# A spectral layer's mode mix split by image half and placed inside the passes of the other half, with one 112-column stationary operand for two image pairs

## The chip, the cores and the metric

The kernel runs on one core of one Trainium2 chip. The metric is the device time of one launch in microseconds (us), as the median of several runs. One further execution was taken with the hardware profiler; all rows below come from it.

## The reference

Four blocks act in turn on 32 images of 8 channels, 64x64: a coupled-map block with a small neural cellular automaton and a gate, a spherical 3x3 convolution, a spectral block (a grouped Fourier neural operator), and a second spherical convolution; the data are normalised between them. The change is almost all in the spectral block, which is this (40 channels, in 4 groups of 10):

```python
h = fc0(x)                                   # 2 channels and 2 coordinates of each group -> 10
for n in range(4):
    xf = jnp.fft.rfft2(h).reshape(Bb, G, WID, Hh, Wf)
    lo = jnp.einsum('bgixy,gioxy->bgoxy', xf[:, :, :, :M1, :M2], w1c)       # rows 0..11, 12 columns
    hi = jnp.einsum('bgixy,gioxy->bgoxy', xf[:, :, :, Hh - M1:, :M2], w2c)  # rows 52..63
    h = gswish(irfft2(lo and hi, zero elsewhere) + grouped 1x1 convolution of h)
out = fc2(gswish(fc1(h)))
```

## The kernel before, in words

`spectral_layers` does the Fourier transforms as matrix products. The 32 images are cut into 8 units of 4 images; a unit is 2 pairs (`S2`) of 2 images (`B2`). A pass is the work on one unit in one layer, and a layer is 8 passes. All five engines run their own written-out order of instructions and meet at semaphores. On TensorE a pass is:

- `pointwise` (L1380): 16 tiles of 4 matmuls. The stationary operand is 128 columns of `chan` (the transposed activations, and rows of the inverse transform in the other direction); the moving one is 96 columns of `cols`, which holds the row-transformed coefficients (partitions 0 to 47) and the 1x1 weights (48 to 127). So the inverse transform over the columns and the 1x1 convolution are one product. ScalarE evicts each tile with the activation (`activate`, L1480) into `act_b`, which has two buffers.
- `forward_rows` (L1434) of the unit before, put behind the first two tiles.
- `inverse_rows` (L1400) of the next unit: 10 tiles of 4 matmuls, each with 48 columns of `coef` (one channel of one image pair) as the stationary operand and `ih`, 128 columns, as the moving one. ScalarE copies each tile of 512 columns into `cols` (`cols_out`, L1489).
- `forward_cols` (L1414): 8 tiles of 5 matmuls, evicted by VectorE.

Every matmul on 32-bit floats stands in the trace as two records.

A layer's modes go to DRAM (`modes`) after each pass. When all 8 passes are done, `mix` (L1442) multiplies them with the weights of the layer: 8 chunks of 3 mode rows, 288 matmuls in all, with 40 stationary columns and 64 moving ones (two parts, 32 images). Even tiles are evicted by VectorE, odd ones by ScalarE, in four instructions each (`PARTS`), into one of two `om` buffers; SyncE stores these to DRAM (`mixed`), and a buffer is written again when its store has landed (`stored`). After the last store SyncE loads the first unit's `coef`, and the next layer begins. During this time SyncE also fills `cols` with the next layer's 1x1 weights by a broadcast transfer (L1338). The chunks of modes lie in the space of `act_b`, so mixing and passes cannot overlap:

```python
for layer in range(LAYERS):
    if layer:
        inverse_rows(layer, 0)
    for u in range(UNITS):
        ...
    forward_rows(layer * UNITS + UNITS - 1)
    pe.wait_ge(a_out, (layer + 1) * UNITS * NZ)
    for n in range(CHUNKS):
        mix(layer * CHUNKS + n)
```

`spectral_head` applies the last inverse transform, fc1 and fc2. A unit there is 16 tiles (`pointwise`, then `hidden` and `project` for earlier tiles); 10 of them also carry a tile of `inverse_rows` for the next unit. The head starts behind a barrier of all engines.

## Time and profile before

| what | us |
|---|---|
| median of 3 runs | 3396.33 |
| lowest and highest | 3392.22, 3400.08 |
| profiled execution, its own time | 3415.88 |
| its span in the trace | 3414.1 |
| TensorE, busy | 2765.8 (81% of the span) |
| VectorE, busy | 1928.0 (56%) |
| ScalarE, busy | 1436.8 (42%) |
| GpSimd, busy | 799.9 (23%) |

Busy time of TensorE counts pipelined matmuls and can overlap, so the distance from one start to a later one is what a group of matmuls costs. The granted clock is given in parts of 2.4 GHz: 1.00 is that, 0.50 is 1.2 GHz. TensorE's mean granted clock over the span is 0.921.

### The profile page before, as it was taken

The page shows a single profiled execution, that of the slowest core. Times are in us where ns is not written, and L with a number is a line of the kernel's source. Part 1 is how long each engine was busy: PE and PEld are TensorE (multiplying, and loading weights), DVE is VectorE, ACT ScalarE, POOL GpSimd, SP SyncE. Part 2 cuts the span into 40 slices and gives each one's busy share as a digit, 9 for nine tenths or more (in the row PEclk, how much of TensorE's full clock was granted, in tenths as well). Part 3 has the DMA queues.
Part 4 walks back from the last instruction along what each step waited for, and adds up shares of the span by engine and source line. Part 5 has one row for each costly group of instructions (what it writes and reads, how often), then busy time and mean ns, then how long its engine had stood idle before and what let it go on. Part 6 is the DMA issues. An engine that isn't in the chain of part 4 may idle for free. (4 is left out here: it accounts for less than half of the span.)

```text
span 3414.1 us, 44327 instructions
## 1 busy us (share of the span) xinstructions
PE 2765.8 (81%) x17128; PEld 2145.9 (63%) x17128; DVE 1928.0 (56%) x2482; ACT 1436.8 (42%) x2425; POOL 799.9 (23%) x717
## 2 busy tenths in 40 slices
PE   0599996859657499579995899779996699999658
PEld 0244443436445499478985889669985687887435
DVE  5988776635535432345445355354553588788643
ACT  1777775632123122243324333253333465665322
POOL 2988601212214121000000000000000144444310
PEclk9999998979878799789998999889998899999879
DMA  9300005569533457867776777668867544342134
GB/s 190 85 9 15 24 0 147 176 140 198 140 90 85 89 131 169 208 170 164 182 185 183 162 183 170 177 154 191 199 151 202 101 71 73 61 69 40 63 90 95
DMA packets 343282, 429.69 MB, mean 126 GB/s; under 512 B 260726, under 2 KB 302326, under 8 KB 317710
## 3 DMA queue, kind: packets, MB, share of 16 engines
q1 hardware_dynamic: 342599, 422.08, 52.2%
q0 software_dynamic: 496, 5.01, 0.4%
q8 instruction: 131, 2.15, 0.3%
q14 instruction: 56, 0.46, 0.0%
HBM read 254.42 MB, written 164.42 MB: 123 GB/s over the span
## 5 line engine op out<-in xcount | busy, mean ns | idle before, releaser
L1177 DVE STREAM_TRANSPOSE spec_chan<-spec_form_in 128x1024 f32<-128x1024 f32 x256 | 491.9, 1945 | 64.5 <-PE fno_pz L1396 64.5
L1487 ACT ACTIVATE fno_act<-fno_pz 128x320 f32<-128x320 f32 x512 | 224.0, 437 | 607.5 <-PE fno_pz L1396 607.5
L1372 POOL TENSOR_SCALAR fno_minus<-fno_both 96x960 f32<-96x960 f32 x32 | 103.7, 3240 | 1344.3 <-DVE fno_both L1587 1344.3
L1579 DVE COPY fno_wfreq<-fno_pw 128x240 f32<-128x240 f32 x256 | 97.6, 395 | 470.2 <-PE fno_pw L1429 468.2
L1396 PEld LDWEIGHTS fno_pz<-spec_cols,spec_chan 128*128 128x128 f32 x3072 | 348.2, 192 | 12.3 <-issue 9.5
L1396 PE MATMUL fno_pz<-spec_cols,spec_chan 128*128 128x96 f32 x3072 | 350.0, 275 | 2.0 <-ACT spec_cols L1495 2.0
L1452 PE MATMUL fno_pz<-fno_act,fno_wt 128*40 128x64 f32 x2304 | 205.9, 264 | 148.9 <-DMA fno_act<-scratch_modes 106.4
L1715 POOL TENSOR_TENSOR head_hact_lo<-head_hact,head_hact_hi 128x512 fp32r<-128x512 f32 x128 | 228.0, 1784 | 401.7 <-DVE head_hact_hi L1862 401.7
L1429 PE MATMUL fno_pw<-fno_fw,fno_act 128*128 128x96 f32 x2560 | 303.4, 277 | 14.4 <-DVE fno_wfreq L1579 8.6
L1429 PEld LDWEIGHTS fno_pw<-fno_fw,fno_act 128*128 128x128 f32 x2560 | 291.4, 192 | 26.9 <-DVE fno_wfreq L1579 14.8
L1452 PEld LDWEIGHTS fno_pz<-fno_act,fno_wt 128*40 128x40 f32 x2304 | 198.2, 139 | 158.9 <-issue 143.5
L609 PE MATMUL cml_acc<-cml_logis,cml_mats 128*128 128x512 f32 x480 | 247.2, 597 | 56.1 <-DVE cml_logis L566 56.1
L1409 PE MATMUL fno_pj<-spec_ih,fno_coef 96*48 96x128 f32 x1920 | 223.9, 280 | 44.6 <-DMA fno_coef<-scratch_mixed 44.6
L611 PE MATMUL cml_acc<-cml_moved,cml_mats 128*128 128x512 f32 x480 | 247.0, 596 | 10.2 <-ACT cml_moved L532 10.2
L1409 PEld LDWEIGHTS fno_pj<-spec_ih,fno_coef 96*48 96x48 f32 x1920 | 206.2, 126 | 58.8 <-DMA fno_coef<-scratch_mixed 45.2
L1812 ACT ACTIVATE head_hact<-head_pw,head_b,spec_rates 128x512 f32<-128x512 f32 x256 | 189.4, 779 | 45.6 <-PE head_pw L1756 22.9
L609 PEld LDWEIGHTS cml_acc<-cml_logis,cml_mats 128*128 128x128 f32 x480 | 91.9, 192 | 171.7 <-issue 115.4
L574 DVE SCALAR_TENSOR_TENSOR cml_grid<-cml_acc,cml_drive 128x512 f32<-128x512 f32 x224 | 154.5, 690 | 77.3 <-PE cml_acc L611 77.0
L1495 ACT ACTIVATE spec_cols<-fno_pj 48x512 f32<-48x512 f32 x240 | 141.8, 591 | 125.3 <-PE fno_pj L1409 125.3
L531 ACT ACTIVATE cml_moved<-cml_logis 64x496 f32<-64x496 f32 x240 | 148.2, 617 | 90.6 <-DVE cml_logis L579 89.1
L1514 ACT ACTIVATE spec_cols<-fno_pz,spec_rates 40x192 f32<-40x192 f32 x192 | 83.8, 610 | 212.1 <-PE fno_pz L1452 178.7
L611 PEld LDWEIGHTS cml_acc<-cml_moved,cml_mats 128*128 128x128 f32 x480 | 91.6, 191 | 126.6 <-issue 86.1
(195 smaller groups left out, 4977.7 us busy)
## 6 DMA issues: line engine op xcount, KB each, us to landing
scratch_form<-fno_act SPq DMA_DIRECT2D x32, 2560.0 KB, 17.2
spec_form_in<-scratch_form SPq DMA_DIRECT2D x64, 1024.0 KB
fno_act<-scratch_modes SPq DMA_DIRECT2D x128, 180.0 KB
nca_raw<-scratch_xnp SPq DMA_DIRECT2D x66, 329.7 KB
fno_coef<-scratch_mixed SPq DMA_DIRECT2D x48, 360.0 KB, 10.8
spec_form_in<-scratch_form SPq DMA_DIRECT2D x32, 512.0 KB
fno_wt<-table_mix_w SPq DMA_DIRECT2D x32, 450.0 KB, 10.7
scratch_modes<-fno_both SPq DMA_DIRECT2D x64, 180.0 KB
```

The costliest lines, as they stand in the source:

```text
L531: nc.scalar.activation(bj(moved[0:64, t, :])[:, :, 0:J - 1], bj(logis[0:64, t, :])[:, :, 1:J], ACT.Copy).then_inc(moved_ready, 1)
L574: nc.vector.scalar_tensor_tensor(out=grid[:, t % 4, :], in0=acc[:, t % BANKS, :], scalar=FLOOR, in1=drive[:, t, :], op0=ALU.max, op1=ALU.a ...
L609: nc.tensor.matmul(acc[:, t % BANKS, :], mats[:, 0, c].rearrange("p s h -> p (s h)"), logis[:, t, :], start=True, stop=False)
L611: nc.tensor.matmul(acc[:, t % BANKS, :], mats[:, 1, c].rearrange("p s h -> p (s h)"), moved[:, t, :], start=False, stop=True).then_inc(sum ...
L1177: return nc.vector.transpose(chan[:, to * TR * PIX:(to + 1) * TR * PIX].rearrange("p (h q w) -> p h q w", h=TR, q=4), src)
L1396: mm = nc.tensor.matmul(pz[:, t % 4, m * 96:(m + 1) * 96], left, cols[:, h * CS:h * CS + 96] if layer else wz[:, :], start=m == 0, stop=Tr ...
L1409: mm = nc.tensor.matmul(pj[0:SB, t % 2, m * 2 * H:(m + 1) * 2 * H], coef[:, g * WID + i, sub * SB:(sub + 1) * SB], ih[:, :], start=m == 0, ...
L1429: mm = nc.tensor.matmul(pw[:, t % 2, m * 2 * SB:(m + 1) * 2 * SB], act_b[:, n % 2, c0:c0 + 2, :].rearrange("p c h -> p (c h)"), fw[:, :], ...
L1452: mm = nc.tensor.matmul(pz[0:CH, n % 4, j * 64:(j + 1) * 64], wt[:, m % WTS, t // 2 * KY + y, :], rows[:, t // 2, :, :].rearrange("p r (a ...
L1487: nc.scalar.activation(act_b[:, n % 2, :, 4 * t:4 * t + 4], z, ACT.Silu if layer else ACT.Copy).then_inc(a_out, 1)
L1715: nc.gpsimd.tensor_tensor(hpart[1][:, n % 2, 1, :], hact[:, n % 2, 1, :], hpart[0][:, n % 2, 1, :].bitcast(F32), ALU.subtract).then_inc(f_ ...
L1812: nc.scalar.activation(hact[:, e % 2, s, :], pw[:, s, :], ACT.Silu, scale=rates[:, 0, 2, 3:4], bias=b1[:, :]).then_inc(f_act, 1)
```

## The change

- **Mix.** The modes are mixed by halves of the batch: 16 images, 4 units. `mix(m)` is now one mode row of one half: 12 matmuls with 40 stationary and 32 moving columns. The first half of a layer (units 0 to 3) is mixed in units 5 and 6 of the same layer; the second half in units 1 and 2 of the next. In such a pass one `mix` stands behind each of the pointwise tiles 3 to 14. Only the second half of the last layer is mixed by itself, at the end. So 14 passes carry 12 `mix` each, and 24 stand at the end.
- **Buffers.** `act_b` has one buffer in place of two; `xm`, `om` and `wt` have their own space. Modes and weights come in chunks of 2 mode rows, 5 in flight; `om` has 4 buffers of one mode row. The mix writes into the two PSUM banks of `pj`, in turn with `inverse_rows`.
- **Stores.** `mixed` is stored by ScalarE's own DMA queue (`store_mixed`), two stores behind every odd row's eviction. Modes go to DRAM for two units at a time.
- **Stationary operand.** `coef` is laid out with the second image pair at column 64, so that one matmul takes 112 columns, both pairs, and `inverse_rows` has 5 tiles in place of 10, here and in the head. ScalarE evicts a tile in two copies of 512 columns, or four of 256 where it crosses a group.
- **Fill.** The 1x1 weights of the next layer are copied into `cols` by GpSimd and ScalarE, half each (2560 columns), in place of the broadcast transfer. ScalarE waits for GpSimd's half before it goes on to `cols_out`.
- **Order of transfers.** In a pass SyncE now issues the store of `act_b` first, then `coef`, then the unit after next; before, the unit came first. In the first spherical convolution the mask is loaded at the start, and the first unit is normalised before the short chain on the `betas`.

```diff
-XC = 3
+XC = 2
 CHUNKS = NX // XC
-WTS, XB = 4, 4
+XB, OB = 5, 4
+PER, MIX_AT = NX // 2, 3
+FH = B * KY // 2
+ST = 64
-NJ, NZ, NW, NH = CS // 8, H // 4, G * S2, 2
+NJ, NZ, NW, NH = CH // 8, H // 4, G * S2, 2
...
-        act_b = ph.sb("act", [128, 2, CS, H])
+        act_b = ph.sb("act", [128, CS, H])
+        xm = ph.sb("xm", [128, XB, XC, 2, FH])
+        om = ph.sb("om", [CH, OB, 2, UNITS * ST])
...
+        def mixed_in(n):
+            q = n // 4 - 1
+            return range(q * NX + PER * (n % 4 - 1), q * NX + PER * (n % 4)) if q >= 0 and n % 4 in (1, 2) else range(0)
...
                     for t in range(NJ):
...
                         for m in range(4):
-                            mm = nc.tensor.matmul(pj[0:SB, t % 2, m * 2 * H:(m + 1) * 2 * H],
-                                                  coef[:, g * WID + i, sub * SB:(sub + 1) * SB], ih[:, :],
+                            mm = nc.tensor.matmul(pj[0:ST + SB, pj_at[user] % 2, m * 2 * H:(m + 1) * 2 * H],
+                                                  coef[:, 4 * t + m, 0:ST + SB], ih[:, :],
                                                   start=m == 0, stop=True, skip_group_check=True)
...
                 def mix(m):
+                    c = m // XC
+                    if m % XC == 0:
+                        pe.wait_ge(wt_in[c % XB], 16 * (c // XB + 1))
+                        pe.wait_ge(x_in[c % XB], 64 * (c // XB + 1))
+                    pj_free(("mix", m))
...
+                    for y in range(KY):
+                        mm = nc.tensor.matmul(pj[0:CH, pj_at["mix", m] % 2, y * 32:(y + 1) * 32], wt[:, c % XB, m % XC * KY + y, :],
+                                              rows[:, :, :, y, :], start=y == 0, stop=True, skip_group_check=True)
+                    mm.then_inc(mix_done, 1)
+
+                for n in range(ALL):
+                    for t in range(NZ):
+                        if t == 2 and n:
+                            forward_rows(n - 1)
+                        pointwise(n, t)
+                        if len(mixed_in(n)) and MIX_AT <= t < MIX_AT + PER:
+                            mix(mixed_in(n)[t - MIX_AT])
+                    if UNITS <= n + 1 < ALL:
+                        inverse_rows(n + 1 - UNITS)
+                    forward_cols(n)
+                forward_rows(ALL - 1)
+                for m in last_mix:
+                    mix(m)
...
+                def mix_out(m):
+                    act.wait_ge(mix_done, m + 1)
...
+                    if m >= OB:
+                        act.wait_ge(stored[m % OB], 16 * (m // OB))
...
+                def store_mixed(m):
+                    act.wait_ge(out_s if m % 2 else out_v, m // 2 + 1)
+                    f = m // NX % 2 * UNITS * ST
+                    act.dma_start(mixed[:, m % NX, :, f:f + UNITS * ST].rearrange("r c f -> c r f"), om[:, m % OB, :, :]).then_inc(stored[m % OB], 16)
+
+                for n in range(ALL):
+                    for t in range(NZ):
+                        activate(n, t)
+                        if len(mixed_in(n)) and MIX_AT <= t < MIX_AT + PER and (t - MIX_AT) % 2:
+                            m = mixed_in(n)[t - MIX_AT]
+                            mix_out(m)
+                            if t - MIX_AT > 1:
+                                store_mixed(m - 3)
+                                store_mixed(m - 2)
...
+                    if n % UNITS == UNITS - 1:
...
+                        nc.scalar.activation(cols[:, COLS // 2:COLS].rearrange("p (h c) -> p h c", c=CS), wide(wsm[:, n // UNITS, :], H // 2, 1), ACT.Copy).then_inc(fill_act, 1)
+                        act.wait_ge(fill_act, n // UNITS + 1)
+                        act.wait_ge(fill_pool, n // UNITS + 1)
+                    if UNITS <= n + 1 < ALL:
+                        cols_out(n + 1 - UNITS)
```

On TensorE this is the end of layer 0 before the change: L1396 is `pointwise`, L1429 `forward_cols`, L1438 `forward_rows`, L1452 `mix` and L1409 `inverse_rows`.

```order
L1396 MATMUL fno_pz<-fno_wz,spec_form_in 128x96 x8
L1438 MATMUL fno_pw<-fno_wfreq,fno_fh 96x480 x4
L1396 MATMUL fno_pz<-fno_wz,spec_form_in 128x96 x56
L1429 MATMUL fno_pw<-fno_fw,fno_act 128x96 x40
L1438 MATMUL fno_pw<-fno_wfreq,fno_fh 96x480 x4
L1452 MATMUL fno_pz<-fno_act,fno_wt 40x64 x288
L1409 MATMUL fno_pj<-spec_ih,fno_coef 48x128 x40
L1396 MATMUL fno_pz<-spec_cols,spec_chan 128x96 x64
```

This is the start of unit 5 in layer 0 after the change, with the first rows of the mix: L1427 is `pointwise`, L1457 `forward_cols`, L1466 `forward_rows`, L1478 `mix`.

```order
L1457 MATMUL fno_pw<-fno_fw,fno_act 128x96 x40
L1427 MATMUL fno_pz<-fno_wz,spec_form_in 128x96 x8
L1466 MATMUL fno_pw<-fno_wfreq,fno_fh 96x480 x4
L1427 MATMUL fno_pz<-fno_wz,spec_form_in 128x96 x8
L1478 MATMUL fno_pj<-fno_xm,fno_wt 40x32 x12
L1427 MATMUL fno_pz<-fno_wz,spec_form_in 128x96 x4
L1478 MATMUL fno_pj<-fno_xm,fno_wt 40x32 x12
L1427 MATMUL fno_pz<-fno_wz,spec_form_in 128x96 x4
```

The block of 288 matmuls behind the layer has become 12 matmuls between pointwise tiles of 4, and each now has half the moving columns.

On ScalarE the mix before the change was a block of its own: L1514 is the eviction of odd tiles, L1495 `cols_out`, L1487 `activate`.

```order
L1514 ACTIVATE spec_cols<-fno_pz,spec_rates 40x6x16x2 x12
L1514 ACTIVATE fno_om<-fno_pz,spec_rates 40x6x16x2 x12
L1495 ACTIVATE spec_cols<-fno_pj 48x128x4 x10
L1487 ACT_TABLE_LOAD
L1487 ACTIVATE fno_act<-fno_pz 128x80x4 x16
```

After the change, in unit 5 of layer 0 (L1509 is `activate`, L1529 `mix_out`, L1536 `store_mixed`):

```order
L1509 ACTIVATE fno_act<-fno_pz 128x80x4 x85
L1529 ACTIVATE fno_om<-fno_pj,spec_rates 40x12x8x2 x4
L1509 ACTIVATE fno_act<-fno_pz 128x80x4 x2
L1529 ACTIVATE fno_om<-fno_pj,spec_rates 40x12x8x2 x4
L1536 DMA scratch_mixed<-fno_om 40x2x512 x2
L1509 ACTIVATE fno_act<-fno_pz 128x80x4 x2
L1529 ACTIVATE fno_om<-fno_pj,spec_rates 40x12x8x2 x4
L1536 DMA scratch_mixed<-fno_om 40x2x512 x2
```

Evictions of the mix and the issue of its stores now stand between the activations of the pass, two tiles apart.

## Rows read from the trace of the kernel before

**Rows 1.** Windows: us, busy PE, PEld, DVE, ACT, POOL (records), clock, DMA share, GB/s.
```profile
1160.00:1380.00 220.00, 215.29 (x1728) 198.64 (x1727) 77.95 (x98) 55.99 (x128) 38.50 (x7) 0.99 0.67 153
1505.00:1788.00 283.00, 278.74 (x2288) 255.59 (x2288) 143.42 (x139) 98.97 (x200) 18.25 (x7) 1.00 0.77 186
...
2580.00:2700.00 120.00, 61.27 (x656) 58.56 (x656) 47.19 (x115) 47.42 (x106) 2.61 (x1) 0.79 0.72 166
```

**Rows 2.** Windows 1380.29 to 1505.38, 1788.14 to 1900.95, 2183.80 to 2297.26: their sum.
```profile
sum 351.36, PE 191.02 PEld 182.71 DVE 143.20 ACT 142.84 POOL 7.82; mean PE 63.67 PEld 60.90 DVE 47.73 ACT 47.61 POOL 2.61
```

**Rows 3.** Timeline of TensorE, one pass of layer 1: start, us, line, xrecords.
```profile
1611.36 1.95 PE L1396 MATMUL fno_pz<-spec_cols,spec_chan 128*128 128x96 f32 x16
...
1628.94 8.96 PE L1409 MATMUL fno_pj<-spec_ih,fno_coef 96*48 96x128 f32 x80
1637.84 4.71 PE L1429 MATMUL fno_pw<-fno_fw,fno_act 128*128 128x96 f32 x40
...
1647.73 1.95 PE L1396 MATMUL fno_pz<-spec_cols,spec_chan 128*128 128x96 f32 x16
```

**Rows 4.** Timeline of TensorE, end of layer 1 to layer 2; in brackets idle and releaser.
```profile
1784.68 3.46 PE L1438 MATMUL fno_pw<-fno_wfreq,fno_fh 128*96 128x480 f32 x8 [0.50 <-DVE fno_wfreq L1579]
1812.03 16.55 PE L1452 MATMUL fno_pz<-fno_act,fno_wt 128*40 128x64 f32 x192 [23.89 <-DMA fno_act<-scratch_modes]
...
1866.52 4.00 PE L1452 MATMUL fno_pz<-fno_act,fno_wt 128*40 128x64 f32 x48 [0.23 <-issue]
1871.12 2.11 PE L1452 MATMUL fno_pz<-fno_act,fno_wt 128*40 128x64 f32 x24 [0.60 <-DVE fno_om L1617]
1888.14 12.13 PE L1409 MATMUL fno_pj<-spec_ih,fno_coef 96*48 96x128 f32 x80 [14.91 <-DMA fno_coef<-scratch_mixed]
```

**Rows 5.** Timeline of TensorE, before the spectral block, granted clock 0.50.
```profile
1118.09 2.34 PE L399 MATMUL sph_acc<-sph_row_sums,sph_mask 96*128 96x32 f32 x10 [6.76 <-DMA sph_mask<-table_gnmask]
```

**Rows 6.** Timeline of all engines while the mix runs, and at its end.
```profile
1827.92 0.70 SPq L1297 DMA_DIRECT2D scratch_mixed<-fno_om  x2
...
1836.78 1.72 ACT L1514 ACTIVATE fno_om<-fno_pz,spec_rates 40x192 f32<-40x192 f32 x4 [2.91 <-DMA scratch_mixed<-fno_om]
...
1874.99 0.67 SPq L1297 DMA_DIRECT2D scratch_mixed<-fno_om  x2
...
1881.66 19.54 SPq L1278 DMA_DIRECT2D fno_coef<-scratch_mixed  x4
```

**Rows 7.** Timeline of ScalarE, back-to-back evictions of 512 columns in an earlier stage.
```profile
642.17 0.60 ACT L748 ACTIVATE nca_hid_hi<-nca_conv 96x512 fp32r<-96x512 f32 x1 [1.38 <-PE nca_conv L724]
642.66 0.67 ACT L742 ACTIVATE nca_out<-nca_point,nca_buc 24x512 f32<-24x512 f32 x1
```

**Rows 8.** Groups by line: busy us, mean ns of one, idle time before and its releaser.
```profile
L1495 ACT ACTIVATE spec_cols<-fno_pj 48x512 f32<-48x512 f32 x240 | 141.8, 591 | 125.3 <-PE fno_pj L1409 125.3
L1372 POOL TENSOR_SCALAR fno_minus<-fno_both 96x960 f32<-96x960 f32 x32 | 103.7, 3240 | 1344.3 <-DVE fno_both L1587 1344.3
L678 POOL CAST nca_win_hi<-nca_raw 121x2110 fp32r<-121x2110 f32 x22 | 44.3, 2013 | 259.8 <-DMA nca_buc<-table_nca_bu 155.7 <-DMA nca_raw<-scratch_xnp 104.2
```

**Rows 9.** Windows of one unit of the head, columns as in the first group.
```profile
2823.00:2886.00 63.00, 61.95 (x364) 51.17 (x365) 50.98 (x77) 38.30 (x57) 26.62 (x17) 1.00 0.38 66
```

**Rows 10.** Timeline of TensorE in the head, tiles without and with `inverse_rows` (L1728).
```profile
2763.28 1.03 PE L1744 MATMUL head_pz<-spec_chan,head_cols 128*80 128x128 f32 x8
...
2766.47 1.03 PE L1744 MATMUL head_pz<-spec_chan,head_cols 128*80 128x128 f32 x8
...
2770.86 1.03 PE L1744 MATMUL head_pz<-spec_chan,head_cols 128*80 128x128 f32 x8
```

**Rows 11.** Timeline of VectorE before the first pass: the `betas` chain, the normalisation.
```profile
1150.92 0.17 DVE L1526 TENSOR_SCALAR fno_work<-fno_work 128x12 f32<-128x12 f32 x1 [13.52 <-DMA fno_wbias<-table_w_bias]
...
1154.81 4.72 DVE L1554 TENSOR_SCALAR spec_form_in<-spec_form_in,fno_norm 16x4096 f32<-16x4096 f32 x2
```

**Rows 12.** DMA issues by line: count, KB each, median us from issue to landing.
```profile
scratch_form<-fno_act SPq DMA_DIRECT2D x32, 2560.0 KB, 17.2
```

480 lines of the change are left out of this document (235 added, 245 removed).

## The prediction

> **What bounds the kernel now.** I read the windows by stage first, then TensorE's timeline, since the change is all between 1160 and 3210 us. In the eight passes of a layer TensorE is busy for 278.7 of 283 us [rows 1]; in the three gaps between layers together for 191 of 351 us, with no other engine above that [rows 2], and for 61.3 of 120 before the head [rows 1]. So a pass costs what TensorE's matmuls cost, and a gap between layers is a chain of waits: modes to DRAM and back (24 us without a matmul), the mix, 15 us until `coef` is there, then `inverse_rows` alone [rows 4]. In the head TensorE is busy for 61.95 of 63 us, VectorE for 51.0 [rows 9].
>
> A pass lasts 1647.73 - 1611.36 = 36.37 us, of which `inverse_rows` takes 1637.84 - 1628.94 = 8.90 [rows 3]: 111 ns for each of 80 records. The profiled execution took 3415.88 us against a median of 3396.33. I make the sum as a difference and take it off the median; by its own execution the result would read 19.5 us more.
>
> **The change, term by term.**
>
> *1. The gaps between layers go.* The second one runs from the end of layer 1's rows (1784.68 + 3.46 = 1788.1) to 1900.95, 112.8 us [rows 2, 4]; measured in the same way, the three hold 351.4 us [rows 2], and all of it goes. The transfer of the 1x1 weights into `cols` goes with them.
>
> *2. `inverse_rows`.* 40 records in place of 80. Does one cost more with 112 stationary columns? The record with 128 of them and 96 moving ones costs the same as this one with 48 and 128: tiles 0 and 1 and the rest of `pointwise` and `forward_cols` fill 27.5 us with 208 such records and 8 of 480 columns, about 0.11 each [rows 3]. So TensorE takes 4.45 us. But ScalarE must evict the same 10 x 512 columns in that time. One copy takes 591 ns [rows 8]; back to back they start 0.49 us apart [rows 7]. With two PSUM banks TensorE's third tile waits for the first two copies (1.0 + 1.1 us), and the fifth for the third tile's four small ones (about 0.35 us apart, my estimate between those rows). Played through, the five tiles take 5.7 us, so a pass gains 8.90 - 5.7 = 3.2 us, not 4.45, and costs 33.2.
>
> *3. The passes together.* Layers 1 and 2: from 282.8 us (the window in [rows 1]: 7 x 36.37 and a last pass of 28.2 without `inverse_rows`) to 8 x 33.2 + 3 = 268.4. Layer 3 has none in its last pass: 7 x 33.2 + 28.2 = 260.4. Layer 0 has no `inverse_rows` before and one after; its 220.6 us (the first window of [rows 1], to the ends of its matmuls) lose the last `forward_rows` with its waits, 4.6, to the next layer's first pass, and get 5.7 + 3: 224.7. The 3 us are the new fill at the end of a layer. ScalarE copies 2560 columns and waits for GpSimd's 2560 before it may evict `inverse_rows`, and TensorE gets only two tiles ahead. GpSimd takes 0.95 ns per column in the cast, 3.4 in the negation [rows 8], so 2.4 to 8.6 us, for a stall of 1.5 to 7.7; I take 3, near the cast, a plain copy too. Nothing but the end of `forward_cols` could hide it, and that stands behind. Change of the passes: -28.8 - 22.4 + 4.1 = -47 us.
>
> *4. The mix inside the passes.* Now it costs TensorE's own time: 14 passes x 12 rows x 24 records = 4032 records, twice as many per layer as before, each with 32 moving columns in place of 64. What does one cost? Groups of 48 and 24 records take 4.00 and 2.11 us, so 1.89 / 24 = 79 ns each at the full clock [rows 4]. If moving columns bound it, 64 of them would take 53 ns at the rate of the pass (8.90 us / 80 / 128 columns = 0.87 ns), so something else does, and halving them should not help. A row with 32 moving and 128 stationary columns agrees: 10 records in 2.34 us at clock 0.50, near twice 0.11 us [rows 5], no cheaper than 96 moving ones. I take 80 ns: 4032 x 0.080 = +323 us. This is the price that eats most of term 1. Bound below: 53 ns, if the stepped moving operand was the limit.
>
> *5. Waits inside the mix.* Four `om` buffers. ScalarE stores rows k-3 and k-2 behind the eviction of row k, and the eviction of row k+2 waits for the store of k-2. One round of two rows is, on TensorE, 2 x (0.90 + 1.92) = 5.63 us. Round the stores it is: issue of two (2 x 0.35 us, as a SyncE issue [rows 6]), landing, four evictions (1.72 us [rows 6]). Landing: the last two stores of the old mix, 720 KB with quiet DMA engines, took 1881.66 - 1875.66 = 6.0 us; in the midst of mode loads on their own queue 1836.78 - 1828.62 = 8.2 us [rows 6]. The new pair is 320 KB, on a queue of its own. I take 3.9 us, since less than half the bytes are nearer to the quiet row, and get 6.3 us, 0.6 more than TensorE's round. The first two rounds of a pass find free buffers, so 14 x 4 x 0.6 = +34 us. Ends: 0, and 2.8 a round (landing 6.0) = +157.
>
> The Trainium skill ("DMA: Bandwidth & Descriptors", Anatomy of one DMA) gives about 2.0 us and the bytes over 436 GB/s for one transfer, which would be under 3 us here and no wait at all, 34 us less. By the rows above the landing is longer, and the sum stays with them.
>
> *6. The end of the mix.* The last half is mixed alone: two rounds at 3.8 us and ten at 6.3, 71 us against 61.5 before (1812.03 to 1873.2 [rows 4]). It starts some 5 us sooner, as the modes no longer share the DMA engines with the fill, and what follows waits for a store of 160 KB, not 720. I set this gap at 120 us as before [rows 1]: 0.
>
> *7. The head.* A tile with `inverse_rows` takes 4.39 us, one without 3.19 [rows 10]: 1.2 us for each of 5 tiles less in 7 units, 42 us. VectorE's 51.0 us a unit then stand against 58 in place of 64, so some waits come back: -37 us (0 to 15 us of them lost).
>
> *8. The start.* TensorE waits 6.76 us for the mask [rows 5], of which some 4.7 go before the sums bind. The `betas` chain of 3.9 us (1150.92 to 1154.81) leaves the path of the first normalisation [rows 11], and perhaps some of the 13.5 us ahead of it; three memsets then stand before the second one. -9 us.
>
> **Costed at nothing.** `act_b` with one buffer: a pass may evict its first tile when the store of the last has landed. The store took 17.2 us [rows 12] behind the unit's load on the queue; now it goes first. TensorE has 5.7 us of `inverse_rows`, 9.9 of `forward_cols`, four tiles and `forward_rows` (6.8) before it needs that buffer, 22.4 us. Without this cover each us of lateness would cost 31 us. Loads of the next unit now start behind that store but have a full pass.
>
> Sum: -351 - 47 + 323 + 34 + 0 - 37 - 9 = **-87 us**, 3396 - 87 = **3309 us**.
>
> **Rivals.**
>
> *A. Cheaper mix records* (chance 0.17, about 3265 us). The Trainium skill ("TensorE: Matmul & The Clock Gate", Back-to-back issue gap and LDWEIGHTS) has no limit near 79 ns for such a matmul: it gives some 25 ns as the floor of a small one, and P/1.2, 33 ns, for 40 weight columns. No row here shows a record below 79. If the stepped operand was the limit, at 53 ns TensorE's round falls to 4.35 us, but the four gated rounds stay at 6.3: a pass gains 2 x 1.3 + 4 x 0.1 = 3 us, in all some 44. Only if stores landed faster too would it be more (to 3240).
>
> *B. Stores gate the mix* (0.12, about 3450 us, the other side). Same mechanism as term 5 with the landing of the quiet row, 6.0 us: a round of 8.4 us, 2.2 more than forecast in 14 x 4 + 10 rounds, +145. The kernel is slower from a landing of about 5.3 us. Against it: half the bytes, own queue. For it: every landing that I can read in the old mix is 6 us or more.
>
> *C. Nothing of the pass is saved and the copies bind elsewhere* (0.08, about 3355 us). The fill at GpSimd's slow rate (+14), the head held by VectorE (+15), the `act_b` store late by half a us in each pass (+16).
>
> *D. The gap's work returns in another way* (0.08, 3390 us and more): mode chunks late for tile 3, since 20 loads and a store stand ahead of them; 5 us in each of 7 first passes, and B in part.
>
> **How the numbers follow.** The forecast (3280 to 3350) has 0.55. Range for 8 in 10: low is A with its full gain, 3240; high is D and the milder part of B, 3390. A measurement here tells about 0.2%, 7 us. Slower by more than that: B without its mild part and the end of D, 0.10; within it 0.02; faster 0.88.
>
> **What would show it.** Passes of 33 us without and 58 with mix, 14 of them; L1478 with 24 records in about 1.9 us between tiles; the time of L1529 waiting for stores, near 0.6 us a round; L1437 taking 5.7 us; TensorE idle once at each layer's end by some 3 us; the head's unit at 59 us. It is wrong if L1478 costs far from 80 ns a record, or if a round of two rows lasts over 7.5 us.

## The result, and the profile after

The changed kernel takes 3364.82 us, median of 5 runs (3358.81 to 3371.63), against 3393.81 for the kernel before (3386.45 to 3400.08): a ratio of 0.991, 95% interval 0.990 to 0.993. That is 29 us less, where 87 were forecast. Its profiled execution took 3364.67 us (span 3362.6), near its median, while that of before lay 20 us above its own: so the two spans differ by 51 us, and 14 of that stand ahead of all that was changed. One execution of one experiment (the first run of the constant rows' semaphore, 3514.8 us) was slow throughout, mean clock 0.79 against 0.89, and is left out of its ratio.

The timeline of TensorE, at the first matmul of the stages: `forward_cols` of unit 0, `pointwise` of layers 1, 2 and 3, and of the head.

```profile
1161.77 9.17 PE L1457 MATMUL fno_pw<-fno_fw,fno_act 128*128 128x96 f32 x80 [0.53 <-ACT fno_act L1509]
...
1473.37 1.95 PE L1427 MATMUL fno_pz<-spec_cols,spec_chan 128*128 128x96 f32 x16
...
1853.86 1.95 PE L1427 MATMUL fno_pz<-spec_cols,spec_chan 128*128 128x96 f32 x16
...
2224.47 1.95 PE L1427 MATMUL fno_pz<-spec_cols,spec_chan 128*128 128x96 f32 x16
...
2698.08 5.27 PE L1793 MATMUL head_pz<-spec_chan,spec_cols 128*80 128x128 f32 x24 [7.97 <-DVE spec_chan L1183]
```

The same view of the kernel before has these marks at 1176.87, 1505.38, 1900.95, 2297.26 and 2700.06. The first stage of the table begins with the wait ahead of the sums with the mask (1111.33 before, 1097.04 after), the head ends with the fourth reduction behind it (3237.66 and 3188.66). In us:

| stage | before | after | change | forecast |
|---|---|---|---|---|
| mask's wait to unit 0's `forward_cols` | 65.5 | 64.7 | -1 | -9 |
| to layer 1 | 328.5 | 311.6 | -17 | -70 |
| layer 1 | 395.6 | 380.5 | -15 | -25 |
| layer 2 | 396.3 | 370.6 | -26 | -26 |
| layer 3 and last gap | 402.8 | 473.6 | +71 | +79 |
| head | 537.6 | 490.6 | -47 | -37 |

Most of what is missing lies in layer 0. But the layers that come out near the forecast do so with other numbers than mine. A pass is the time between two `forward_rows`. Without mix it takes 33.42 us (1663.96 - 1630.55 in the rows below; forecast 33.2):

```profile
1630.55 3.39 PE L1466 MATMUL fno_pw<-fno_wfreq,fno_fh 128*96 128x480 f32 x8
1633.77 12.64 PE L1427 MATMUL fno_pz<-spec_cols,spec_chan 128*128 128x96 f32 x112
1646.25 1.93 PE L1437 MATMUL fno_pj<-spec_ih,fno_coef 96*112 96x128 f32 x16
1648.69 1.13 PE L1437 MATMUL fno_pj<-spec_ih,fno_coef 96*112 96x128 f32 x8 [0.52 <-ACT spec_cols L1517]
1650.02 1.13 PE L1437 MATMUL fno_pj<-spec_ih,fno_coef 96*112 96x128 f32 x8 [0.20 <-ACT spec_cols L1517]
1651.44 1.13 PE L1437 MATMUL fno_pj<-spec_ih,fno_coef 96*112 96x128 f32 x8 [0.29 <-ACT spec_cols L1517]
...
1663.96 3.39 PE L1466 MATMUL fno_pw<-fno_wfreq,fno_fh 128*96 128x480 f32 x8
```

Beside them stand the five tiles of `inverse_rows`: from 1646.25 to the start of `forward_cols` some 6.1 us, with waits for ScalarE's copies (forecast 5.7, before 8.90, [rows 3]).

Passes with mix were forecast at 58 to 59 us, all alike. In layers 1 to 3 the first of each pair takes 65.0 to 69.7 us and the second 50.0 to 53.9. Here is the first mix pass of layer 1 on three engines, from the first row of the mix on:

```profile
1513.63 1.14 PE L1478 MATMUL fno_pj<-fno_xm,fno_wt 128*40 128x32 f32 x24
1514.71 1.13 PE L1427 MATMUL fno_pz<-spec_cols,spec_chan 128*128 128x96 f32 x8
1515.77 1.14 PE L1478 MATMUL fno_pj<-fno_xm,fno_wt 128*40 128x32 f32 x24
...
1521.23 0.76 ACTq L1536 DMA_DIRECT2D scratch_mixed<-fno_om  x2
...
1531.41 1.61 DVE L1651 TENSOR_SCALAR fno_om<-fno_pj,spec_rates 40x192 f32<-40x192 f32 x4 [8.91 <-DMA scratch_mixed<-fno_om]
1533.16 1.78 PE L1478 MATMUL fno_pj<-fno_xm,fno_wt 128*40 128x32 f32 x24 [6.66 <-DVE fno_om L1651]
1534.87 2.02 PE L1427 MATMUL fno_pz<-spec_cols,spec_chan 128*128 128x96 f32 x8
1536.83 1.81 PE L1478 MATMUL fno_pj<-fno_xm,fno_wt 128*40 128x32 f32 x24
...
1555.15 8.91 PE L1437 MATMUL fno_pj<-spec_ih,fno_coef 96*112 96x128 f32 x40
```

At first a row takes 1514.71 - 1513.63 = 1.08 us, 45 ns for each of 24 records, not 80, and row and tile together 2.13 us. Then VectorE waits 8.9 us for the first store (issued at 1521.2, landed at 1531.4), and TensorE 6.66 us for VectorE. Behind the wait a row takes 1.71 us and row and tile 3.67, to the end of the mix, and the `inverse_rows` behind it still take 8.7 us in place of 6.1. The windows of that stretch say why (us, busy PE, PEld, DVE, ACT, POOL, clock, DMA share, GB/s):

```profile
1513.00:1533.00 20.00, 13.51 (x199) 12.47 (x197) 10.12 (x17) 6.55 (x17) 2.33 (x1) 0.90 0.94 200
1533.00:1559.00 26.00, 25.84 (x210) 24.62 (x211) 6.68 (x14) 10.17 (x25) 0.00 (x0) 0.50 0.47 145
1581.00:1608.00 27.00, 25.14 (x381) 23.39 (x380) 16.43 (x28) 12.96 (x33) 2.43 (x1) 1.00 0.52 130
```

The granted clock falls to 0.50 (1.2 GHz) in the course of the wait and is there for all 26 us of the second window, which ends behind the last mix row. The third row is the mix of the pass after, with two waits of 0.7 and 1.1 us: clock 1.00. The DMA engines are at 0.94 in the stretch in which the first stores land, and at 0.52 in the later one.

How late a store of `mixed` lands can be read only where an eviction waited for it. Here it is 1531.41 - 1521.23 = 10.2 us behind its issue, and 9.4 to 10.2 us in all six of these passes for the first store. In the second passes and in the mix at the end it is 2.6 to 5.5 us, as here (ScalarE issues two, VectorE waits for the first):

```profile
1604.08 0.68 ACTq L1536 DMA_DIRECT2D scratch_mixed<-fno_om  x2
1606.71 1.62 DVE L1651 TENSOR_SCALAR fno_om<-fno_pj,spec_rates 40x192 f32<-40x192 f32 x4 [2.73 <-DMA scratch_mixed<-fno_om]
```

I had taken 3.9 us for all.

In layer 0 there is more. This is VectorE and TensorE in unit 5, from the first mix rows on:

```profile
1288.51 1.14 PE L1478 MATMUL fno_pj<-fno_xm,fno_wt 128*40 128x32 f32 x24
...
1298.62 4.72 DVE L1575 TENSOR_SCALAR spec_form_in<-spec_form_in,fno_norm 16x4096 f32<-16x4096 f32 x2 [13.24 <-DMA spec_form_in<-scratch_x]
...
1305.19 1.78 PE L1478 MATMUL fno_pj<-fno_xm,fno_wt 128*40 128x32 f32 x24 [14.47 <-DVE fno_om L1651]
```

VectorE's first eviction of the mix stands behind the normalisation of unit 6, whose images SyncE loads behind 20 loads of modes. TensorE idles 14.5 us, and again the clock is at half for the rest of the mix: the two mix passes of layer 0 take 74.7 and 65.2 us, against 27.2 without mix. And in the last pass of the layer `forward_cols` stops in the middle:

```profile
1444.83 4.60 PE L1457 MATMUL fno_pw<-fno_fw,fno_act 128*128 128x96 f32 x40
1464.77 1.89 DVE L1183 STREAM_TRANSPOSE spec_chan<-spec_form_in 128x1024 f32<-128x1024 f32 x1 [17.12 <-DMA spec_form_in<-table_iw_t]
1467.01 6.52 PE L1457 MATMUL fno_pw<-fno_fw,fno_act 128*128 128x96 f32 x40 [17.57 <-DVE fno_wfreq L1628]
```

VectorE waits for the constant rows of the inverse transform (`iw_t`) in the `form_in` buffers, and its column copies stand behind that. In the kernel before, the same loads were issued 10 us and more ahead of the gap and needed only behind it, so the gap covered them.

So the trace of one execution accounts for the result thus. Over plain passes of the same layers, the 14 mix passes cost 395 us (forecast 357); the last pass of layer 0 holds 17.6 us of waiting that I had at 0.

### The profile page after: what moved, and what is told of

Same layout as the page of the kernel before. It is cut to its first block and busy times, and to the rows that moved or that the text cites. A ratio compares the mean times of both kernels' runs of the same rounds, so it can differ in the third digit from the quotient of the medians.

```text
span 3362.6 us, 46970 instructions
## 1 busy us (share of the span) xinstructions
PE 2772.0 (82%) x18152; PEld 2160.5 (64%) x18152; DVE 1927.8 (57%) x2488; ACT 1445.5 (43%) x2493; POOL 796.7 (24%) x721
## 5 line engine op out<-in xcount | busy, mean ns | idle before, releaser
L1509 ACT ACTIVATE fno_act<-fno_pz 128x320 f32<-128x320 f32 x512 | 225.2, 441 | 729.6 <-PE fno_pz L1427 729.3
L1427 PE MATMUL fno_pz<-spec_cols,spec_chan 128*128 128x96 f32 x3072 | 416.6, 292 | 0.0
L1393 POOL TENSOR_SCALAR fno_minus<-fno_both 96x960 f32<-96x960 f32 x32 | 83.4, 2606 | 1348.1 <-DVE fno_both L1635 1348.1
L1427 PEld LDWEIGHTS fno_pz<-spec_cols,spec_chan 128*128 128x128 f32 x3072 | 388.8, 204 | 18.6 <-issue 10.8
L1478 PE MATMUL fno_pj<-fno_xm,fno_wt 128*40 128x32 f32 x4608 | 269.2, 228 | 101.7 <-DVE fno_om L1651 79.9
L1457 PE MATMUL fno_pw<-fno_fw,fno_act 128*128 128x96 f32 x2560 | 318.5, 286 | 31.3 <-DVE fno_wfreq L1628 27.1
L1457 PEld LDWEIGHTS fno_pw<-fno_fw,fno_act 128*128 128x128 f32 x2560 | 309.1, 201 | 40.2 <-DVE fno_wfreq L1628 32.7
L1478 PEld LDWEIGHTS fno_pj<-fno_xm,fno_wt 128*40 128x40 f32 x4608 | 247.6, 148 | 124.0 <-issue 114.4
L1651 DVE TENSOR_SCALAR fno_om<-fno_pj,spec_rates 40x192 f32<-40x192 f32 x376 | 152.6, 516 | 270.2 <-DMA scratch_mixed<-fno_om 161.9
L1529 ACT ACTIVATE fno_om<-fno_pj,spec_rates 40x192 f32<-40x192 f32 x384 | 156.7, 557 | 194.9 <-PE fno_pj L1478 108.8
L1427 PE MATMUL fno_pz<-fno_wz,spec_form_in 128*128 128x96 f32 x1024 | 145.6, 307 | 36.4 <-DVE spec_form_in L1575 26.5
L1437 PE MATMUL fno_pj<-spec_ih,fno_coef 96*112 96x128 f32 x960 | 148.4, 314 | 28.8 <-ACT spec_cols L1517 28.7
```

Source lines behind the costliest of these rows:

```text
L1427: mm = nc.tensor.matmul(pz[:, t % 4, m * 96:(m + 1) * 96], left, cols[:, h * CS:h * CS + 96] if layer else wz[:, :], start=m == 0, stop=Tr ...
L1457: mm = nc.tensor.matmul(pw[:, t % 2, m * 2 * SB:(m + 1) * 2 * SB], act_b[:, c0:c0 + 2, :].rearrange("p c h -> p (c h)"), fw[:, :], start=m ...
L1478: mm = nc.tensor.matmul(pj[0:CH, pj_at["mix", m] % 2, y * 32:(y + 1) * 32], wt[:, c % XB, m % XC * KY + y, :], rows[:, :, :, y, :], start= ...
L1509: nc.scalar.activation(act_b[:, :, 4 * t:4 * t + 4], z, ACT.Silu if n >= UNITS else ACT.Copy).then_inc(a_out, 1)
L1529: op = nc.scalar.activation(om_tile(m, ri, v), acc_tile(m, part), ACT.Copy, scale=rates[0:CH, 2 if sign > 0 else 3, 1, layer:layer + 1])
L1651: op = nc.vector.tensor_scalar(o, z, by, None, ALU.mult)
```

## The experiments

Each is an edit to the changed kernel, and every ratio is to the kernel before, taken on the same chip. The changed kernel itself gave 0.991 on one chip and 0.994 on another (last group).

### What waits and what the clock does

**Stores at once.**

```diff
-                            if t - MIX_AT > 1:
-                                store_mixed(m - 3)
-                                store_mixed(m - 2)
+                            store_mixed(m - 1)
+                            store_mixed(m)
...
```

> One edit to the changed kernel: each pair of mixed rows is stored right behind the eviction of its odd row, not two tiles (4.3 us) later. In the trace of the changed kernel the first mix pass of each half lasts 65.0 to 68.8 us and the second 50.0 to 53.9; in the first, TensorE idles 5.9 to 6.7 us for a row whose om buffer waits for its store, and from there on the granted clock is 0.50 to the end of the pass. Theory 1 (the idle time itself lowers the clock): the idle time falls to about 2.4 us, as short ones do in the second passes without a change of clock, and the first passes of layers 1 to 3 come down to about 52.5 us: six times 15, about 3275 us. Rival (the low column count of the mix lowers the clock, the wait is a bystander): only the wait shrinks, six times 4.3, about 3339 us, and the clock still falls in the first passes.

3321.5 us, ratio 0.978 (0.975 to 0.981). The waits shrank less than expected, to 3.4 to 5.6 us in layers 1 to 3, and the clock still fell behind each; the first passes took 58.2 to 67.9 us. A store that is issued some 4 us sooner also lands later behind its issue, the first of a pass 11.1 to 13.4 us in place of 9.4 to 10.2, which is why so little of the wait went. It decides nothing between the two, since a wait of 4 us may do what one of 6 does.

**Six `om` buffers, four chunks.** `XB, OB = 4, 6`.

> One edit to the changed kernel: six om buffers, and four mode chunks in flight in place of five, since no more space is left. The stores are issued when they were. The first row that needs a used buffer is two tiles later. Theory 1 (stores gate the first mix pass, and the idle time lowers the clock): idle time for om in the first pass about 2.4 us in place of 6.4, clock 1.00, about 3275 us. Rival (mix itself lowers the clock): about 3339 us. A second rival: the fifth chunk was needed, and TensorE now waits for modes instead, about 3365 us or more.

3288.1 us, 0.967 (0.964 to 0.970). For the first time there are first mix passes at the full clock, of 50.0 and 51.4 us. But now two second passes take 59 to 60: they wait 2.1 and 3.6 us for mix weights, and the clock falls there. The second rival is right in part, the first is in doubt.

**Normalisation behind the mix** in units 5 and 6.

```diff
-                    if n + 1 < UNITS:
-                        normalise(n + 1)
                     outs = mixed_in(n)[0::2]
+                    if n + 1 < UNITS and not outs:
+                        normalise(n + 1)
...
                     for m in outs[3:]:
                         mix_out(m)
+                    if n + 1 < UNITS and outs:
+                        normalise(n + 1)
```

> One edit to the changed kernel: in units 5 and 6 of layer 0 VectorE normalises the next unit behind its evictions of the mix, not ahead of them. In the trace of the changed kernel the first eviction of the mix in unit 5 waits until the unit of images is there (13.2 us) and the normalisation is done (4.7 us): TensorE idles 14.5 us, in unit 6 5.3 us, and in both the clock is 0.50 until the mix ends (passes of 74.7 and 65.2 us against 27.2 without mix). Theory: unit 5 keeps only the wait for the om stores and the low clock (about 62 us), unit 6 runs at full clock (about 46 us), forward_cols of both starts some 3 us late behind the normalisation: together about -26 us, 3339 us. Rival (the low clock comes from the mix, not from the wait): only the waits go, about 3352 us.

3346.8 us (3325 to 3369), 0.983 (0.977 to 0.988): 23 us below 0.991 of the kernel before by the medians, 30 by the ratio, for a forecast of 26. In its trace the two passes take 58.0 and 44.7 us in place of 74.7 and 65.2, 37 less; the second one has no wait and keeps its clock. Three second passes of later layers fell to the low clock in that execution (61.7 to 63.4 us, two of them behind waits of only 1.3 us), which took some of it back.

**All three together** (`XB, OB = 4, 6`).

> Three edits of before together: six om buffers with four chunks in flight, stores right behind each odd row's eviction, normalisation behind the mix in units 5 and 6. Theory (idle time in a mix pass lowers the clock, and low it stays until the mix of the pass ends): no wait for om is left; where no row waits over 1.5 us the pass runs at clock 1.00 in 49 to 50 us, 14 of them; waits for the mix weights (2 to 3.6 us in two passes of the run with six buffers) may still drop two or three. About 3250 us (3220 if none drops). Rival (the clock falls by itself in mix passes): passes of 57 to 60 us stay without any wait, 3285 us.

3283.8 us, 0.967, no better than six buffers alone. But it splits the passes cleanly. The waits of over 1.6 us in layers 1 to 3 are nine, all for mix weights:

```profile
1493.63 1.81 PE L1478 MATMUL fno_pj<-fno_xm,fno_wt 128*40 128x32 f32 x24 [2.64 <-DMA fno_wt<-table_mix_w]
1551.22 1.81 PE L1478 MATMUL fno_pj<-fno_xm,fno_wt 128*40 128x32 f32 x24 [2.12 <-DMA fno_wt<-table_mix_w]
```

The nine passes that hold them take 57.6 to 62.9 us, the three without one 49.0, 49.8 and 49.8. No pass without a wait is slow there: the rival falls for mix rows of this shape (for smaller ones see the price of a record below). And four chunks in flight are too few.

**Eight buffers in the space of four.** Odd rows go to partitions 64 to 103 of `om`, so five chunks stay; normalisation behind the mix, stores when they were.

```diff
-XB, OB = 5, 4
+XB, OB = 5, 8
...
-        om = ph.sb("om", [CH, OB, 2, UNITS * ST])
+        om = ph.sb("om", [ST + CH, OB // 2, 2, UNITS * ST])
...
```

> The changed kernel with eight om buffers in the space of four (odd rows are evicted to partitions 64 to 103, even ones to 0 to 39), five chunks in flight as before, stores issued when they were, and the normalisation of units 6 and 7 behind the mix. In the run with six buffers and four chunks each mix pass without a wait above 1.5 us took 49.0 to 49.8 us at clock 1.00, and each with a wait of 1.7 to 3.9 us for mix weights took 57.6 to 62.9 us. With five chunks those weights were never waited for. Theory (only an idle time lowers the clock): 14 passes of 49 to 51 us (43 to 45 in layer 0), about 3215 us. Rival (five chunks and eight buffers only move the wait to some other transfer, since the DMA engines are 90 to 97% busy there): waits of 2 us and more go on, 3260 to 3285 us.

3219.0 us, ratio 0.948 (0.946 to 0.950), 4 us from the forecast and 5% below the kernel before. Eight of the twelve mix passes in layers 1 to 3 take 48.4 to 49.9 us; here are such a one and the next in windows, and the wait that lies in the second:

```profile
1626.00:1675.00 49.00, 47.04 (x547) 42.45 (x547) 28.63 (x44) 22.89 (x51) 2.61 (x1) 1.00 0.96 249
1675.00:1733.00 58.00, 55.67 (x546) 51.45 (x544) 28.41 (x43) 23.70 (x53) 2.61 (x1) 0.82 0.83 204
```

```profile
1703.71 1.56 PE L1478 MATMUL fno_pj<-fno_xm,fno_wt 128*40 128x32 f32 x24 [2.17 <-DMA fno_wt<-table_mix_w]
```

Two microseconds of waiting cost ten. The busier DMA engines (0.96) are no burden where nothing waits. Four of the 14 passes still fall.

**A pause by design** on this kernel: `pause(n)` is n memsets of a spare tile on VectorE, each behind the one before.

```diff
+                    if m in (30, 54, 78, 102, 126, 150):
+                        pause(28)
...
+                        if t == 3 and n in (12, 16, 20, 24):
+                            pause(28)
```

> The kernel with eight om buffers, and in the first and the second layer-half's mix passes (six in all, behind the sixth row's eviction) and in forward_cols of four plain passes VectorE first does 28 small memsets, one after another, some 5 to 7 us, so that TensorE idles 3 to 5 us by design. Theory (idle time lowers the clock, and the mix keeps it low): each of the six passes gets the idle time and about 9 us more at clock 0.50 to its last mix row; the four plain passes lose the idle time and at most 3 us more. Rival (the low clock is a thing of transfers or of the place in the pass): the paused passes get only their idle time.

One run, 3310.6 us. The pause came out at 7.9 us of TensorE's time in the mix and 8.3 in `forward_cols`:

```profile
1631.60 6.27 PE L1459 MATMUL fno_pw<-fno_fw,fno_act 128*128 128x96 f32 x30 [8.30 <-DVE fno_wfreq L1630]
...
1669.64 1.78 PE L1480 MATMUL fno_pj<-fno_xm,fno_wt 128*40 128x32 f32 x24 [7.93 <-DVE fno_om L1661]
```

```profile
1639.00:1661.00 22.00, 22.00 (x282) 18.96 (x281) 16.36 (x28) 9.85 (x24) 2.61 (x1) 1.00 0.70 176
1670.00:1698.00 28.00, 28.00 (x202) 27.12 (x201) 5.16 (x11) 11.55 (x24) 0.00 (x0) 0.55 0.60 190
1698.00:1704.00 6.00, 5.57 (x49) 5.25 (x47) 5.91 (x8) 0.00 (x0) 0.00 (x0) 1.00 1.14 204
```

The six mix passes with a pause take 63.5 to 67.1 us against 48.4 to 48.8: the 7.9 and 7 to 11 more, at a clock near 0.50 from within the pause to some 5 to 15 us beyond the last mix row. The plain passes take 43.6 to 44.4 against 33.4: the 8.3 and 2 to 3 more. So a wait is followed by the low clock in both places, and among mix rows the clock stays low about three times as long. That is the changed kernel's first mix pass, made at will.

### What the stationary operand does

**Two times 48 columns in place of 112.**

```diff
-                            mm = nc.tensor.matmul(pj[0:ST + SB, ...],
-                                                  coef[:, 4 * t + m, 0:ST + SB], ih[:, :],
+                            for at in (0, ST):
+                                mm = nc.tensor.matmul(pj[at:at + SB, ...],
+                                                      coef[:, 4 * t + m, at:at + SB], ih[:, :],
```

> One edit to the changed kernel: inverse_rows in the layers issues for each channel two matmuls with 48 stationary columns (columns 0 and 64 of coef) in place of one with 112; tiles, evictions and the head stay as changed. 80 records in place of 40 in each of 24 passes. Theory (TensorE's records set its time until ScalarE's copies bind): inverse_rows is again about 8.9 us and a plain pass 36.4 in place of 33.4 us, 24 x 3.0 = +72 us against the changed kernel, about 3442 us. Rival (ScalarE's copies of the same size set it alone): under +20 us.

3355.7 us, 0.989 (0.986 to 0.991): no loss at all. A plain pass takes 33.7 us. The expectation was wrong, and the rows show how:

```profile
1481.20 1.95 PE L1438 MATMUL fno_pj<-spec_ih,fno_coef 96*48 96x128 f32 x32
1483.68 1.08 PE L1438 MATMUL fno_pj<-spec_ih,fno_coef 96*48 96x128 f32 x16 [0.52 <-ACT spec_cols L1518]
1485.01 1.08 PE L1438 MATMUL fno_pj<-spec_ih,fno_coef 96*48 96x128 f32 x16 [0.24 <-ACT spec_cols L1518]
```

Sixteen records take 1.08 us where eight with 112 columns took 1.13: twice as many at half the price. So it isn't that ScalarE hides them; they are cheaper. In [rows 3] a record of the same size took 111 ns, but there each follows one with the same output rows.

**The same, grouped by output rows.**

> As the run with 48 stationary columns, but the four matmuls with output rows 0 to 47 of a tile come first, then the four with rows 64 to 111, in place of turns. With turns, 16 records took 1.08 us, as 8 records with 112 columns did. Theory (a record of 128 columns takes 111 ns behind one with the same output rows, as in the kernel before, and two with different output rows overlap): 16 records take 1.7 to 1.8 us, inverse_rows 8.9 us or somewhat less, plain passes 35.5 to 36.4 us, about 3420 us. Rival (48-column records cost 55 ns here anyway, whatever the order): 33.7 us, 3356 us.

One run, 3372.2 us. Plain passes take 35.0 us, and 32 records 2.51 in place of 1.95:

```profile
1492.27 2.51 PE L1440 MATMUL fno_pj<-spec_ih,fno_coef 96*48 96x128 f32 x32
1495.21 2.88 PE L1440 MATMUL fno_pj<-spec_ih,fno_coef 96*48 96x128 f32 x32 [0.43 <-ACT spec_cols L1520]
```

The order matters, so the theory holds: records in turns on output rows 0 to 47 and 64 to 111 are cheaper. But it matters by 1.3 us a pass, not 3, and the mean record takes at most 2.51 / 32 = 78 ns here, not 111. The starts of the single records in the traces show why. In the kernel before they lie 109 ns apart. In turns, two records with different output rows start 6 or 7 ns apart and the next two 103 ns later, so they run side by side. Grouped, records on the same output rows lie 109 ns apart as before, and only where one group ends and the next begins do the two kinds run side by side.

### What a record of the mix costs

```diff
+                    kind = m // NX % 4
+                        wide_y = 16 if kind == 2 else 32
+                        out_c = 20 if kind == 3 else CH
+                        moving = (rows[:, :, :, y, :] if kind in (0, 3) else plain[:, :, y * 16:(y + 1) * 16] if kind == 1
+                                  else plain[:, 0, y * 16:(y + 1) * 16])
```

> What one record of the mix costs, and why, in four forms by half of a layer, on the changed kernel; three of the four leave the right result out (they read other columns, or half of them). Form 0, as it is: 32 moving columns read in runs of 2; form 1: 32 in runs of 16; form 2: 16 columns in one run; form 3: as form 0, but 20 stationary columns in place of 40. The trace of the changed kernel shows 44 ns a record (24 in 1.07 us) at the full clock and 71 at half. If the stepped reading is the limit, form 1 is below 44 ns; if the number of moving columns is, form 2 is near half; if loading the weights is, form 3 is lower; if it is a fixed cost of an instruction, all four stay at 44.

One run, 3380.0 us. A row and the tile behind it, for forms 1, 2, 3 and 0, all at the full clock:

```profile
1511.56 1.11 PE L1484 MATMUL fno_pj<-fno_xm,fno_wt 128*40 128x32 f32 x24
1512.59 1.13 PE L1427 MATMUL fno_pz<-spec_cols,spec_chan 128*128 128x96 f32 x8
...
1700.81 1.09 PE L1484 MATMUL fno_pj<-fno_xm,fno_wt 128*40 128x16 f32 x24
1701.83 1.13 PE L1427 MATMUL fno_pz<-spec_cols,spec_chan 128*128 128x96 f32 x8
...
1901.32 1.13 PE L1484 MATMUL fno_pj<-fno_xm,fno_wt 128*20 128x32 f32 x24
1902.37 1.13 PE L1427 MATMUL fno_pz<-spec_cols,spec_chan 128*128 128x96 f32 x8
...
2079.61 1.14 PE L1484 MATMUL fno_pj<-fno_xm,fno_wt 128*40 128x32 f32 x24
2080.68 1.13 PE L1427 MATMUL fno_pz<-spec_cols,spec_chan 128*128 128x96 f32 x8
```

24 records take 1.03, 1.02, 1.05 and 1.07 us: 42 to 45 ns each, whatever the reading, the columns or the weights. In these four forms it is a fixed cost. From 64 moving columns (79 ns, [rows 4]) to 32 it nearly halves, and from 32 to 16 it hardly moves.

The run shows something on the clock that I had not asked for. With 16 moving columns (form 2) it fell in both second passes, though no wait in them was longer than 1.1 us. Here is the longest wait of the later pass and the window behind it, and then the first mix row behind a wait with 20 stationary columns (form 3), and a window of more such rows:

```profile
2537.40 1.06 PE L1484 MATMUL fno_pj<-fno_xm,fno_wt 128*40 128x16 f32 x24 [0.60 <-DVE fno_om L1657]
2540.00:2571.00 31.00, 31.00 (x216) 30.02 (x214) 5.99 (x15) 13.64 (x29) 0.00 (x0) 0.50 0.51 163
...
1918.09 1.44 PE L1484 MATMUL fno_pj<-fno_xm,fno_wt 128*20 128x32 f32 x24 [6.10 <-DVE fno_om L1657]
1923.00:1932.00 9.00, 8.35 (x129) 7.66 (x128) 4.48 (x12) 4.69 (x13) 0.00 (x0) 1.00 0.60 185
```

So smaller mix rows lost the clock almost without a wait, which is what the first experiment's rival said. And rows with 20 stationary columns had it back some 4 us behind a wait of 6.1 us, while there was still mix to do. What the mix rows are counts beside the waits. This is one execution, with each form in its own layers, and was not tried further.

### Constant rows, the start, and a better kernel

**A semaphore for each buffer's constant rows.**

```diff
-                        if n == UNITS:
-                            dve.wait_ge(iw_in, 64)
+                        if UNITS <= n < UNITS + 2:
+                            dve.wait_ge(iw_in[n - UNITS], 32)
```

> One edit to the changed kernel: the constant rows of the inverse transform that SyncE loads into the two form_in buffers have a semaphore each, so the first transposition of layer 1 no longer waits for those of the second buffer, which are issued one pass later. In the trace of the changed kernel VectorE waits 17.1 us for them, and TensorE 17.6 us in the middle of forward_cols, because the column copies stand behind that transposition on VectorE. Theory: these 17 us go, about 3348 us. Rival: the first unit itself (its three loads) or its own constants are late too, and under 5 us go.

3368.2 us, 0.991 (0.988 to 0.994), as without the edit. It was run again, next to the changed kernel, for a trace that can be read beside the others.

> The edit of the separate semaphores alone, once more, beside the changed kernel itself on the same chip; the first run with it gave 3368 us where 3348 was expected, and its profile can't be compared with the others (TensorE slower in all passes). With the other edits it was worth 17.6 us in the last pass of layer 0 (56.6 to 39.0 us). Theory: alone it is worth the same in that pass, and the total comes out 10 to 18 us below the changed kernel's. Rival: the units of images, the mix weights and the mode loads shift, and a mix pass or two of layer 1 is longer by what was gained.

> The changed kernel itself, for comparison on one chip with the two runs beside it: 0.991 of the kernel before, 3364 us.

3357.2 us (0.991, 0.989 to 0.994) beside 3372.6 (0.994, 0.993 to 0.996): 15 us less. In the traces the last pass of layer 0 goes from 53.9 to 38.1 us, 15.8 less, layer 1's first mix pass from 68.4 to 75.3. The wait is the semaphore's, and part of what it frees may come back in the next mix. The first run is within what two chips differ by.

**The `betas` chain ahead of the memsets.**

> One edit to the changed kernel: on VectorE the chain on the betas stands directly behind the normalisation of the first unit, and the three memsets of the mix's tiles (12.2 us in the trace of the changed kernel) stand behind it and behind the normalisation of the second unit. There ScalarE's two betas activations and with them its first activate came only at 1147.0, and TensorE idled 9.98 us after two thirds of a pass's first tiles. Theory: about 10 us go, 3360 us beside the changed kernel's 3370 (taken on the same scale as the 3399 of the kernel before on this chip). Rival: the betas themselves arrive late, or the memsets now delay the column copies of the first unit by as much: 0.

3362.9 us, 0.991 (0.988 to 0.993). The 9.98 us wait for ScalarE is gone, but 11.5 us of waiting for a column copy (`fno_wfreq`) stand in `forward_cols` in its place, behind the same memsets. The rival holds.

**All edits.**

> The kernel with eight om buffers, and with three edits of runs before: stores right behind each odd row's eviction, a semaphore for each buffer's constant rows, the betas chain ahead of the three memsets. The stores should cost nothing and gain nothing where no row waits. The constant rows: 13 to 17 us of TensorE's idle time in the last pass of layer 0; the run with that edit alone came out at 0.991 of the kernel before, where the changed kernel stood, so by that nothing, by its trace up to 15 us. The betas edit alone gave 3 us of 8 at most. Theory: 10 to 18 us below the kernel with eight buffers, about 3200 us. Rival: what is freed in layer 0 comes back as a wait for the first unit's coefficients or its rows, and it is within 5 us of it.

3200.8 us, 0.945 (0.943 to 0.947). The last pass of layer 0 takes 39.0 us in place of 56.6, which is the whole difference. Three mix passes still take 57 to 60 us, behind waits for weights.

> The kernel with all four edits, and SyncE issues a chunk's mix weights ahead of its modes, not behind. In the run with all edits three mix passes still wait 2.7, 3.0 and 4.7 us for mix weights (and take 57.3 to 59.8 us in place of 49), where the four mode loads ahead of them took up to 5.6 us to issue. Theory: the weights start 1.4 to 5.6 us sooner, one at most of the three waits is left, about 3178 us. Rival: the modes, now issued later, are waited for in their place, or the DMA engines are the limit: 3200 us within 5.

3199.8 us, 0.944 (0.942 to 0.946): the same. Four waits of 3.0 to 4.9 us remain, three of them now without a named releaser where the modes are waited for next. So the order of the issues isn't the limit; whether the DMA engines are was not tried apart.

## Why the prediction was wrong

The sign and the range were right, the size was not: 29 us against 87. By the steps:

- **Term 1, the gaps:** right, but for 17.6 us in layer 0. I let every wait of the gap go with it. The load of the constant rows had lain under the first gap, and I never asked what else did. With a semaphore of its own the wait is gone (e3b_iw, e12_all).
- **Terms 2 and 3, `inverse_rows` and the passes:** a plain pass 33.4 us for 33.2; the stall by the fill is a wait of 2.3 us for 3, and makes its pass 2.9 to 4.8 us longer, as the clock falls for a moment behind it. That ScalarE's copies bind is right too. But "the record with 128 of them and 96 moving ones costs the same as this one" led me to think that only wider operands help: two 48-column ones in turns do as well (e6_48).
- **Term 4, the price of a record:** 45 ns, not 80, and 52 with what it does to the tiles. The sentence that failed is "so something else does, and halving them should not help". It takes off nearly half, and only below 32 columns does the fixed cost show (e7_price): the starts of single records lie 80 ns apart with 64 moving columns and 40 with 32. The row that seemed to agree ([rows 5], 10 records in 2.34 us at clock 0.50) has 128 stationary columns; with 40, the half clock gives 71 ns here. I kept the nearest row by shape, and none of the rows had fewer columns and fewer weights at once; rival A's 53 ns was the better number. A mix pass without a wait costs 48.4 - 33.4 = 15.0 us over a plain one, where I had 23.0 + 2.4. The rows themselves are 13 us of it. The rest is a cost that no step had: a pointwise tile takes 1.06 us between mix rows (1515.77 - 1514.71) and 0.89 where tiles follow each other (1646.25 - 1633.77 for 14). Per record this comes to 15.0 / 288 = 52 ns. That it meets rival A's 53 is chance, since A took the stepped reading for the limit, and without the steps (form 1 of e7_price) a record costs the same.
- **Term 5, the waits:** 3.9 us for the landing was near in the second passes and the mix at the end (2.6 to 5.5), and far off for the first store of a first mix pass (9.4 to 10.2). There the step from fewer bytes to a shorter landing failed. The DMA engines are near full then (share 0.92 to 0.98 over the six stretches from that store's issue to its landing, about 0.3 where a store landed in 2.6 us), which may be why. That is rival B's mechanism, for a part of the stores. Its result isn't B's, since the rows are cheap and in a second pass TensorE's wait is about 1 us.
- **What no step had:** a wait among mix rows is followed by the granted clock of 0.50, mostly to some 4 to 16 us beyond the last mix row, and this costs 6 to 11 us beyond the wait itself in the experiments (e8_no_stalls, e11_om8, e10_pause) and 10 to 14 in the changed kernel's first passes. In the traces all waits of 1.4 us or more among rows of this shape do this, and some of those of 1.2 to 1.4. In layers 1 to 3 the first mix passes average 67.6 us and the second 50.9, against 48.4. It is luck that their mean, 59.2, is near my 58.6. This is why layers 2 and 3 look right: two errors of opposite sign.
- **Layer 0:** there the waits outweigh the cheap rows. The mix's evictions stood behind a normalisation that waits for images, 14.5 and 5.3 us, with the low clock behind both: 85.5 us for two passes in place of 51 (e4_norm_late). I had listed what is queued behind ScalarE's waits, but not what the mix is queued behind on VectorE.
- **Term 6:** the last gap is 107 us for 120, since the mix by itself takes 52 us and not 71 (the old one is 61.2 by its rows, not 61.5). **Term 7:** -47 for -37, VectorE does not bind in the head. **Term 8:** -1 for -9: the memsets of the mix's tiles took the chain's place (e5_start).

Summed over the trace: 14 x 15.0 = 210 us for the mix itself where 323 were forecast, and 185 us of waits and low clock where 34 were. So the steps that failed are the price of a record in term 4, the first landing in term 5 with the fall of the clock that no term had, and the waits of layer 0 that were put at nothing. With most of the latter removed, the same change is worth 173 us in place of 29 (e11_om8, 0.948).

That waits among rows of this shape lower the clock, and that it then stays low through the mix, is shown by the pause and by the passes with and without a wait. What it is about the rows that keeps it low is open; e7_price shows only that their size matters. That the first stores land late because the DMA engines are full is only argued, from the windows.

## What to carry to other kernels

Small matmuls put between large ones were cheap here as long as nothing waited; a short wait among them cost two to six times its length, because TensorE's clock fell and rows of this shape didn't bring it back (those with half the stationary columns did). So look first at what each engine does ahead of the moved work, and give the first pieces enough buffers that the first landing is covered. When a gap is removed, list everything that lay under it, waits on shared semaphores too.
